# A mixture-of-experts tail on one core: batch 6's experts start every seven steps instead of every six

## The reference, cut to what matters

```python
x = x + _mla(_rmsnorm(x, g1), Wq, Wdkv, Wuk, Wuv, Wo)
h = _rmsnorm(x, g2)                                # t = h as (tokens, 128)
logits = t @ gate_w                                # 128 -> 8 experts
top_v, top_i = jax.lax.top_k(logits, 2)
gates = jax.nn.softmax(top_v, axis=-1)             # scattered into combine (T, 8)
hid = jax.nn.silu(jnp.einsum('td,edh->teh', t, w1))   # every expert, 128 -> 256
ye = jnp.einsum('teh,ehd->ted', hid, w2)              # every expert, 256 -> 128
out = jnp.einsum('te,ted->td', combine, ye)
```

## Time and profile before

| | us |
|---|---|
| median of 3 runs | 1957.47 |
| lowest and highest run | 1955.97, 1969.35 |
| the profiled execution | 1974.12 |
| its span | 1972.3 |
| TensorE busy in the span | 1737.1 (88%) |
| VectorE busy | 1428.1 (72%) |
| ScalarE busy | 1000.2 (51%) |
| GpSimd busy | 625.6 (32%) |
| mean granted TensorE clock | 0.946 |

### The profile page before, as it was taken

The page is one execution under the profiler, slowest core; times in us unless marked ns, Lnnn a source line. Parts: engine busy times, 40 slices in busy tenths (PEclk is TensorE's granted clock), DMA queues, the critical chain, the costliest instruction groups (busy, mean ns, idle before and its releaser), DMA issues.

```text
span 1972.3 us, 46460 instructions
## 1 busy us (share of the span) xinstructions
PE 1737.1 (88%) x17489; PEld 1159.2 (59%) x17489; DVE 1428.1 (72%) x4507; ACT 1000.2 (51%) x2018; POOL 625.6 (32%) x871
## 2 busy tenths in 40 slices
PE   3898889898939479989999999999999999998997
PEld 2676767777726346545655655655555555655455
DVE  6777877787721267877887886887887787788756
ACT  2554455455513146647546636646645645644642
POOL 3111221111134147625514613613623522530000
PEclk6999999999969779979999999999999999999999
DMA  4522122211018222122212213123122122221111
GB/s 120 179 74 70 33 59 79 75 46 38 8 32 262 72 87 89 45 69 77 71 61 88 71 57 102 51 71 101 42 78 76 62 77 75 70 68 61 50 33 50
DMA packets 109933, 144.31 MB, mean 73 GB/s; under 512 B 18752, under 2 KB 90880, under 8 KB 108432
## 3 DMA queue, kind: packets, MB, share of 16 engines
q1 hardware_dynamic: 76576, 113.28, 18.5%
q10 hardware_dynamic: 30128, 18.49, 3.2%
q0 software_dynamic: 3008, 9.57, 1.4%
HBM read 112.89 MB, written 28.15 MB: 72 GB/s over the span
## 4 chain that ended last, share of the span: by engine, by line
PE 51%; DVE 11%; issue 3%; ACT 2%; DMA 1%; SPq 1%; ACTq 1%; POOL 1%; DVEq 0%; POOLq 0%
PE ps L1969 10%; PE ps L1954 8%; PE ps L2110 6%; PE ps L2008 5%; PE ps L2124 5%; PE ps L2019 4%; PE ps L1979 3%; DVE ps L2198 2%; PE ps L1225 2%; PE ps L1234 1%; DVE l_XY L2198 1%; PE ps L1981 1%; PE ps L2059 1%; DVE l_xn L2236 1%; PE ps L2039 1%
## 5 line engine op out<-in xcount | busy, mean ns | idle before, releaser
L1773 POOL TENSOR_SCALAR l_XY<-l_XY,l_nmax 128x512 f32<-128x512 f32 x512 | 388.8, 768 | 224.3 <-DVE l_nmax L2198 215.8
L2198 DVE CUSTOM_DVE_ANT_0 l_XY<-ps,strips 128x512 f32<-128x512 f32 x512 | 341.1, 687 | 140.6 <-PE ps L1954 136.8
L1954 PE MATMUL ps<-l_stack 72*128 72x512 bf16 (+3 forms) x1024 | 353.9, 351 | 65.7 <-DVE l_nmax L2198 53.8
L1830 ACT ACTIVATE PT<-ps 128x512 f32<-128x512 f32 x512 | 305.1, 599 | 197.4 <-PE ps L1969 184.7
L1969 PE MATMUL ps<-ident,l_XY 128*128 128x128 f32 x2048 | 319.0, 278 | 3.8 <-POOL l_XY L1773 3.0
L1969 PEld LDWEIGHTS ps<-ident,l_XY 128*128 128x128 f32 x2048 | 240.3, 141 | 110.5 <-ACT PT L1830 45.5
L2198 DVE CUSTOM_DVE_ANT_0 ps<-ps,mask 128x384 f32<-128x384 f32 (+3 forms) x512 | 245.2, 504 | 31.0 <-PE ps L1954 27.0
L1954 PEld LDWEIGHTS ps<-l_stack 72*128 72x128 bf16 x1024 | 102.0, 100 | 148.6 <-DVE l_nmax L2198 84.3
L1979 PE MATMUL ps<-l_stack 75*128 75x256 bf16 (+3 forms) x512 | 157.7, 310 | 13.1 <-ACT PT_odd L1838 6.0
L1838 ACT ACTIVATE PT_even<-ps 128x512 f32<-128x512 f32 (+1 forms) x256 | 120.9, 493 | 67.2 <-PE ps L1981 56.7
L2110 PE MATMUL ps<-l_fT,l_w_e 128*128 128x512 f32 x256 | 146.0, 659 | 2.6 <-DVE l_hid L2386 1.2
(11 more groups left out here) (309 smaller groups left out, 3051.7 us busy)
## 6 DMA issues: line engine op xcount, KB each, us to landing
l_stack<-parts_dram SPq DMA_DIRECT2D x384, 96.0 KB
stack<-parts_dram SPq DMA_DIRECT2D x48, 384.0 KB
l_w_e<-in_L_ffn_w_dram ACTq DMA_DIRECT2D x128, 128.0 KB
strips<-bias_dram SPq DMA_DIRECT2D x8, 1792.0 KB, 7.4
parts_dram<-l_parts SPq DMA_DIRECT2D x32, 384.0 KB, 2.5
parts_dram<-parts SPq DMA_DIRECT2D x16, 384.0 KB, 6.9
strips<-bias_dram POOLq DMA_DIRECT2D x12, 448.0 KB, 10.0
w_e<-in_L_ffn_w_dram SPq DMA_DIRECT2D x12, 256.0 KB, 6.1
```

What stands on the lines that cost most here:

```text
L1773: nc.gpsimd.tensor_scalar(XY[:, c % XY_BUFS], XY[:, c % XY_BUFS], -1.0, nmax[:, c % 8:c % 8 + 1], ALU.mult, ALU.add).then_inc(y_pool, 1)
L1830: nc.scalar.activation(PT[:, quad(u, r), j], src.rearrange("p (k q) -> p k q", q=P), ACT.Exp).then_inc(moved, 1)
L1954: nc.tensor.matmul(ps[:, n % 3, 0:w], stack[0:STACK, 0, h, q * P:(q + 1) * P], stack[0:STACK, 1, h, 0:w], start=True, stop=True).then_inc( ...
L2198: nc.vector.tensor_tensor_reduce(out=dst, in0=src, in1=add, scale=-1.0, scalar=3.0e38, op0=ALU.add, op1=ALU.min, accum_out=low).then_inc(s ...
```

## The change: seven steps between the experts of batch 6

stages(b) gives batch 6 its own table, equal to STAGES except each=7. Hidden product f of expert e then stands at step 1010 + 7e + 2f (before: 1010 + 6e + 2f), output half u at 1019 + 7e + 2u (before: 1019 + 6e + 2u). Expert 0 stays where it is, expert 7 moves seven steps: its hidden products from 1052 and 1054 to 1059 and 1061, its output halves from 1061 and 1063 to 1068 and 1070, its sums from 1063 and 1065 to 1070 and 1072, and the final addition from 1066 to 1073. Batch 7 still starts at 1062, and batches 0 to 5 keep their table. The number of instructions of every kind is the same.

```diff
@@ -1291,9 +1291,12 @@
                    combine=12, first=8, each=2, second=0, tanh=1, mul=1, ye=3, half=0, sum=2)


+NEXT_TO_LAST = dict(STAGES, each=7)
+
+
 def stages(b):

-    return STAGES if b < B - 1 else LAST_STAGES
+    return STAGES if b < B - 2 else NEXT_TO_LAST if b == B - 2 else LAST_STAGES
```

## The result

The changed kernel takes 1971.51 us (median of 4 runs, 1970.82 to 1977.33) against 1957.63 us before (4 runs): a ratio of 1.0064, 95% interval 1.0042 to 1.0087, or 12.6 us more (8 to 17). Repeated on another chip, where the kernel before had a median of 1968.64 us, the ratio was again 1.0064 (1.0048 to 1.0080). The forecast was 1968 and a loss of 10 us. The profiled execution of the changed kernel took 1972.09 us.

A forecast was written before the change was run, and what follows sets the result against it. TensorE was taken as the bound. A +2.8, B +5.0, C -0.3 and D +2.5 us summed to +10 us, 1967.5 on the median (centre 1968); 1962 to 1971 had 62%, the 8-in-10 range was 1957 to 1976.

The forecast's parts named there:

- the rival with one more low stretch: Another stretch of low TensorE clock, mainly ahead of Wo, costs 3 to 5 us more: 1971 to 1975; 16% chance.
- A: Steps 1024 to 1052: a wait in nearly every hand-over, +2.8 us; -2.9 if all covered, some 5 if none.
- the piece behind the first sum: Batch 7's experts after its first sums: expected to run as before, with late weights priced at nothing.
- D: Batch 7's turning to its first sums: moved output halves, sums and final addition cost +2.5 us, from +1 to +5.
- B: Step 1052 to the product with Wo: no attention left to cover hand-overs, +5.0 us, from +0.5 to +7.
- C: Wo to batch 7's turning: addition waits longer, final addition leaves; -0.3 us, between -0.8 and +0.3.
- the waits are covered: Ahead of Wo, TensorE's work shrinks and the 4.09 us gap absorbs it: -2, or -4 if D cost nothing; 15%.
- The clock falls once more: Another low clock stretch, mainly in B, costs 3 to 5 us more: 1971 to 1975, or 1977 with a second; 16%.

The follow-up runs named there:

- e1: The changed kernel with every output half of batch 6 one step later (ye=10 for 9); 0.9979 of the kernel before.
- e2: The kernel before, six steps between experts kept, with batch 6's output halves one step earlier (ye=8 for 9); 1.0072 of the kernel before.
- e4: The changed kernel with ScalarE's issue of the next weights two steps later for batch 6; 1.0071 of the kernel before.
- e3: The kernel before with only the two output halves of batch 6's last expert and their sums seven steps later; 1.0012 of the kernel before.
- e9: The changed kernel with output halves one step later for batch 6's experts 5 to 7 alone; 1.0025 of the kernel before.
- e5: The changed kernel with output halves one step later for batch 6's experts 0 to 4 alone; 1.0022 of the kernel before.
- e6: The kernel before with 14 matmuls nobody reads in TensorE's 4.09 us gap ahead of batch 7's turning; 0.9999 of the kernel before.
- e7: The changed kernel with batch 6's output halves one step later and 10 unread matmuls in the gap ahead of batch 7's turning; 0.9983 of the kernel before.
- e8: e1 plus the last expert's hidden products and the previous expert's output halves in the gap between Wo and batch 7's turning; 0.9975 of the kernel before.

## Why the prediction was right, point by point

- *The sign, the size and the main cause* were right: a loss of 10 us was forecast, nearly all of it by uncovered hand-overs, 12.6 were measured, and e1 and e2 show the cause from both sides. The whole lies within 1% of before, as forecast. The median of 1971.51 is inside the range of 8 in 10 (1957 to 1976), but 0.5 us above the 1962 to 1971 that had 62%, and just inside the 1971 to 1975 of the rival with one more low stretch. In the stretches, against a forecast of 10.0 us the profiled execution has 13.5 (the repeat 13.8): A and the piece behind the first sum came out larger than forecast, D in that execution smaller.
- *A, steps 1024 to 1052, +2.8:* the mechanism was right and the size too small. Measured +5.5 between the hidden products, 1871.16 to 1907.20 (36.0 against 30.5 us); +4.1 in the repeated change at the full clock. The mis-sized term is the three steps of attention between an expert's last output half and the next hidden product. I took 1.4 us. For example, from the output half at 1895.20 in the changed kernel to the hidden product at 1898.13 are 2.93 us, of which 0.95 is the half: 2.0 us, because the exponentials wait for TensorE, then for the weight issue, and TensorE for them. The issue's share is 1.7 us in all (e4). The rest of A's loss in the profiled execution is the low clock from 1900.71 on, some 1.4 us by the difference to the repeated change (36.68 against 35.25). The upper bound, "some 5", was wrong by the prediction's own prices: eight hand-overs of 1.67 us on top of the attention, less the 2.9 us of moved work, are +10.5, so that 2.8 was not near the upper end. The first two of these rows (the third is shown above):

```profile
1871.16 1.12 PE L2113 MATMUL ps<-l_fT,l_w_e 128*128 128x512 f32 x2
...
1895.20 1.16 PE L2127 MATMUL ps<-l_w_e,l_hid 128*128 128x128 f32 x8
```

- *B, to Wo, +5.0:* measured +4.85, step by step where the working had put it: output half 2.62 behind the start at 1907.20 (2.63 expected), turning of the attention output at 7.0 (7.15), turning of the divided output at 9.5, Wo at 11.9 (12.1). In e1, with these hand-overs covered, the stretch is 8.81 us and not 12.26.
- *C, to the turning, -0.3:* measured -0.5.
- *D, to the first sum, +2.5:* +0.5 in the profiled execution, +3.1 in the repeated change, +2.6 in e3. The size was right where the clock stays low; in the profiled execution it had come back by 1928.53, which the lower end of +1 had for its reason, and +0.5 lies below even that.
- *Behind the first sum, 0:* **this step failed.** I let batch 7's experts run as before; the stretch is 3.2 us longer (2.3 in the repeat, 1.7 in e3). With batch 6's final addition directly ahead of batch 7's multiplication on VectorE, the idle time ahead of the sixth product grew from 1.25 to 2.16 us, and the clock fell behind it (windows above): output halves and hidden products from 1940.60 took 3.75 and 2.41 us for 2.02 and 1.88, which is 2.3 of the 3.2 us. I priced the final addition on the way to the first sum, but not on the bank that the sixth product waits for. In e1 and e9, where it stands behind that multiplication, the stretch is as before (27.42 and 27.38), so the cost is one of place. The low clock has not this cause alone: in e2, whose batch 7 runs in the order of before, it fell at the same operation (3.56 us for 2.02). A wait of 0.66 us for weights at 1959.51 (0.37 in the repeat) can't be put down to the change: e3, e4 and e5, with the same order there, have none, and e6, in the order of before, has 0.77.
- *Ahead of step 1024*, where the sum begins, no price was set: +0.3 us (+0.15 in the repeat).
- *The rivals:* "the waits are covered" is what e1 makes true: A is -2.9 as worked out, B +1.4 for the +0.5 worked out, and the time 4 us less than before. The -4 of the prediction doesn't follow from its terms, though: A at -2.9, B at +0.5 and C at -0.3 without D are -2.7. "The clock falls once more" came true in the profiled execution, in A and behind the first sum, but not in B, where I mainly put it: B kept 1.00 in the repeat at 9.08 us busy of 13, e2 at 8.12 of 12. By the Trainium skill ("TensorE: Matmul & The Clock Gate", section "A second HAM failure mode: psum-queue depth-cycling") frequent short idle times made the clock of one kernel swing between its levels; in e2 the trace disagrees over 50 us of them, in A of the changed kernel it agrees once, and once in A of e9 (2.05 us for an output half at 1905.43), while the repeat of the change kept 1.00 over nearly the same waits.
- What stays open: whether a low stretch behind the first sum comes with every execution of the change (it did in both profiled ones, with stretches 3.2 and 2.3 us longer, and in e3, e4 and e5), what brings it, and how much of 1.0064 it makes. All stretches are from one or two executions of each kernel. The windows of the repeated change show the full clock ahead of Wo, and 0.82 around the first sum:

```profile
1881.00:1916.00 35.00, 27.79 (x195) 1.00 0.09 27
1916.00:1929.00 13.00, 9.08 (x56) 1.00 0.14 41
1948.00:1956.00 8.00, 4.45 (x19) 0.82 0.26 74
```

## What to carry to other kernels

In an order written by hand, the distance that counts is from an operation to whoever needs its result through other engines, not from one unit of work to the next: measure that hand-over once (here 1.67 us from the end of TensorE's product over ScalarE and VectorE back to TensorE), and keep so much work between the two on the waiting engine. Spacing units out thins the cover of every hand-over, so the second distance has to grow with the first. An idle gap elsewhere takes moved work in only if the work stands ahead of the gap's end in program order, and what it costs is read up to the end of the launch. Where trailing work of one unit meets the next unit on another engine, one step can decide: here the final addition ahead of a multiplication or behind it.

## What the runs showed of the hardware that was not expected

TensorE busy for only 80% of 38 us, with idle times up to 1.3 us, kept a granted clock of 1.00 (e2). Single idle times give no rule either: around the first sum, two of 2.2 and 0.85 to 1.5 us were followed by 0.50 in e3 and in both executions of the change, and two of 0.59 and 1.47 us in e2, where the kernel before kept 1.00 behind 1.25 and 1.46; e1, e7 and e9 kept 1.00 through 1.2 and 1.95 us, and e8 lost it behind the same two. Between two executions of the same change the clock differed too: 0.50 at 1902 to 1904 in the one, 1.00 in the other over nearly the same waits. Holding the clock up by filler matmuls made the same transposes 1.7 times faster, 0.63 for 1.08 us, and the stretch behind 2.8 us shorter, but no change of the launch's time that could be measured.
